# A transformer tower on one Trainium2 core: every turn of a tile by DMA, the weight preparations at other places of tile 0, and a new fixed order on all five engines

## The reference

```python
h = _L0_tok_ref(x, ...)                                  # three table rows summed, layernorm
h = h + _L0_attn_ref(_layernorm(h), ...)                 # linear attention, 16 heads, random features
h = h + _L0_ffn_ref(_layernorm(h), ...)                  # 32 prototypes, the two nearest give low-rank maps
h = h + _L1_attn_ref(_layernorm(h), ...)                 # causal softmax attention with rotary positions
h = h + _L1_ffn_ref(_layernorm(h), ...)                  # 256 -> 1024 -> 256 with ternary weights
return h
```

## Time and profile before

| | us |
|---|---|
| median of 3 runs (499.96 to 501.84) | 500.15 |
| the profiled execution | 500.82 |
| its span in the trace | 499.1 |
| TensorE busy | 394.7 |
| VectorE busy | 359.6 |
| ScalarE, GpSimd busy | 267.4, 253.5 |

### The profile page before, as it was taken

How to read it: one execution, slowest core, us unless ns; L and a number is a source line. 1 busy time by engine, 2 the same in 40 slices (tenths; PEclk the granted TensorE clock), 3 DMA queues, 4 the chain that set the end, 5 groups by cost and what they waited for, 6 DMA issues and landing times.

```text
span 499.1 us, 11429 instructions
## 1 busy us (share of the span) xinstructions
PE 394.7 (79%) x3771; PEld 262.3 (53%) x3800; DVE 359.6 (72%) x989; ACT 267.4 (54%) x579; POOL 253.5 (51%) x342
## 2 busy tenths in 40 slices
PE   3245646477889898999989999999898989868774
PEld 1032433345566564666666667666675756535432
DVE  4365479789879886889888988989796877544241
ACT  1315454154848675757667586858575655522330
POOL 6733505475757765656757485756353443411100
PEclk9765558679989997999999999999999999998899
DMA  4815904137667578767976878866978687446053
GB/s 112 253 34 167 272 11 84 32 69 123 102 110 145 103 132 158 99 127 150 161 140 141 131 156 143 169 130 134 148 120 139 111 126 131 88 96 122 16 78 93
DMA packets 194139, 60.58 MB, mean 121 GB/s; under 512 B 185696, under 2 KB 191488, under 8 KB 194080
## 3 DMA queue, kind: packets, MB, share of 16 engines
q1 hardware_dynamic: 192496, 55.52, 60.0%
q0 software_dynamic: 1584, 4.33, 3.1%
HBM read 11.85 MB, written 2.36 MB: 28 GB/s over the span
## 4 chain that ended last, share of the span: by engine, by line
PE 32%; DMA 16%; issue 15%; DVE 15%; POOL 14%; ACT 5%; SPq 3%; POOLq 0%; ACTq 0%; DVEq 0%
PE PS L1270 10%; DMA rTm<-split 6%; DVE split L960 3%; PE PS L1650 3%; DMA mT<-stage_r 3%; PE PS L1692 2%; PE PS L1605 2%; POOL qe L547 2%; DMA xTM<-xsM 2%; DMA xTo<-xso 2%; DMA qkT<-qs 2%; PE PS L1425 1%; PE PS L1593 1%; PE PS L1332 1%; POOL hres L509 1%
## 5 line engine op out<-in xcount | busy, mean ns | idle before, releaser
L1044 ACT ACTIVATE xnR<-hres,nmeanR,rstdR 128x256 f32<-128x256 f32 x16 | 9.6, 600 | 58.9 <-DVE nmeanR L937 58.9
L960 DVE TENSOR_REDUCE split<-PS 128x16 f16<-128x2048 f32 x16 | 36.7, 2292 | 4.9 <-PE PS L1583 4.9
L1650 PE MATMUL PS<-w1q,xTM 128*128 128x512 f16 x128 | 34.3, 392 | 2.9 <-DVE xTM L1008 1.7
L1692 PE MATMUL PS<-w2q,mT 128*128 128x256 f16 x256 | 31.6, 278 | 4.7 <-DMA mT<-stage_r 4.7
L1519 PE MATMUL PS<-faT_hi,hgT 128*128 128x256 f16 x128 | 24.9, 282 | 8.9 <-issue 6.3
L1280 PE MATMUL PS<-proj_hi,qkT 128*128 128x176 f16 x128 | 24.8, 256 | 7.8 <-DMA qkT<-qs 4.7
L1692 PEld LDWEIGHTS PS<-w2q,mT 128*128 128x128 f16 x256 | 24.4, 99 | 10.8 <-issue 3.7
L1270 PE MATMUL PS<-wqkT_hi,xTP 128*128 128x512 f16 x64 | 25.2, 437 | 5.5 <-DVE xTP L781 3.3
L569 POOL TENSOR_TENSOR rstdR<-rstdR,consts 128x1 f32<-128x1 f32 x16 | 8.7, 545 | 37.2 <-DVE rstdR L933 37.2
L565 POOL TENSOR_TENSOR hgs<-hg,hgs 128x512 f16<-128x512 f32 x16 | 20.8, 1298 | 12.3 <-ACT hgs L1041 12.3
L576 POOL TENSOR_TENSOR stage_f<-stage_f 128x512 f32<-128x512 f32 x16 | 20.3, 1267 | 12.9 <-DVE stage_f L955 9.4
(11 more groups left out here) (306 smaller groups left out, 1375.4 us busy)
## 6 DMA issues: line engine op xcount, KB each, us to landing
out<-outb SPq DMA_DIRECT2D x16, 128.0 KB, 2.6
w<-in_w1T SPq DMA_DIRECT2D x1, 1024.0 KB, 7.4
w<-in_w2T SPq DMA_DIRECT2D x1, 1024.0 KB, 7.8
stage_p<-in_wqkT SPq DMA_DIRECT2D x1, 512.0 KB
stage_f<-in_fbT SPq DMA_DIRECT2D x1, 512.0 KB, 4.3
stage_f<-in_faT SPq DMA_DIRECT2D x1, 512.0 KB, 4.6
stage_r<-in_rwqk SPq DMA_DIRECT2D x1, 512.0 KB, 3.9
rT<-split SPq DMA_TRANSPOSE x32, 3.3
```

Source lines behind the costliest of these rows:

```text
L960: v.tensor_reduce(slots(48)[:, 0:H, 0].rearrange("p (c j) -> p j c", j=4), PS[:, BANK["mk1"]:BANK["mk1"] + 4, :].rearrange("p j (c k) -> p ...
L1650: pe.matmul(dst, xT["M"][:, n, :], w1q[:, n % KC, cols], start=(n == 0), stop=False)
L1692: pe.matmul(PS[:, BANK["m2"], 0:D], mT[:, j, :], w2q[:, j % FC, :], start=(j == 0), stop=False)
```

## The change

The turns by TensorE at P, o, r and M are taken out with their copies (24 operations), and 24 operations of the way by DMA come in for them, on the same eight (place, tile) pairs. All numbers of the order are new, and so are the PSUM banks: `qk`, `o`, `wo`, `m2` and `pvT` share bank 2, while `Rtr`, `rqk`, `of`, `y` and `v` share bank 7; `m1`, `fK`, `fh` and `pvx` meet in banks 0 and 1, `fQ` has 4 and 5. On VectorE `setup_p` comes right behind the first normalisation of tile 0's embedding, `setup_o1` behind `Pnm` of tile 0, `setup_o2` and `setup_f1` behind its `diag`; on ScalarE `setup_o` and `setup_f` come behind `sq`, `setup_m` behind `onh`; on TensorE `setup_o2` comes behind `v` of tile 0.

```diff
-START = (2.13016, 6.2721, 10.48426, ...
+START = (12.38286, 17.45035, 22.53895, ...
 ...
-    "qk": 5, "kmxT": 2, "kbc": 2, "fK": 0, "v": 7, "ctx": 7, "fQ": 0, "o": 6,
-    "of": 7, "Ftr": 2, "prt": 0, "fh": 1, "y": 2, "Rtr": 7, "rqk": 7, "rv": 2,
-    "mk1": 3, "pvx": 6, "pvT": 2, "wo": 7, "m1": 3, "m2": 7, "Ptr": 4, "ont": 3,
-    "Mtr": 0, "rot_": 2,
+    "qk": 2, "kmxT": 6, "kbc": 6, "fK": 0, "v": 7, "ctx": 6, "fQ": 4, "o": 2,
+    "of": 7, "Ftr": 3, "prt": 3, "fh": 0, "y": 7, "Rtr": 7, "rqk": 7, "rv": 1,
+    "mk1": 3, "pvx": 0, "pvT": 2, "wo": 2, "m1": 0, "m2": 2,
 }
...
-BY_PE = {
-    "P": (0,), "o": (0, 1, 15), "M": (14, 15),
-    "r": (14, 15),
-}
...
-def taken(op, t):
-    if op in FOR_PE:
-        return t in BY_PE[FOR_PE[op]]
-    return op not in FOR_DMA or t not in BY_PE[FOR_DMA[op]]
...
     v.tensor_scalar(nmean["E"][:, :], mv["E"][:, 0:1], rstd["E"][:, 1:2], -1.0, ALU.mult, ALU.mult)\
         .then_inc(nm_ok["E"], 1)
+    if t == 0:
+        setup_p()
...
     if t == 0:
-        setup_p()
         setup_o1()
-        setup_o2()
...
     v.tensor_reduce(diag[:, :], sq[:, :, :], AX_X, ALU.add).then_inc(diag_ok, 1)
     if t == 0:
+        setup_o2()
         setup_f1()
```

More of the change, by code:

```diff
@@ L148, in place @@
         return START[t] + STRETCH[t] * PLACE[op][0 if t < FIRST else 2 if t >= LAST else 1]
-    return sorted(((op, t) for op in ENGINE[engine] for t in range(TILES) if taken(op, t)), key=lambda x: (place(*x), x[1]))
+    return sorted(((op, t) for op in ENGINE[engine] for t in range(TILES)), key=lambda x: (place(*x), x[1]))
 def wait(eng, sem, count):
@@ L1335, in step @@
             def step(op, t):
-                if op == "Ptr":
-                    wait(pe, xn_ok["P"], t + 1)
-                    free("T_P", T_ok["P"], 16 * t)
-                    free("ml2_ok", ml2_ok, issued["m1"])
-                    free("ex1_ok", ex1_ok, issued["mk1"])
-                    for c in range(KC):
-                        last = pe.transpose(PS[:, BANK["Ptr"], c * P:(c + 1) * P], xn["P"][:, c * P:(c + 1) * P], ident[:, :])
-                    last.then_inc(lo_ok["P"], 1)
-                    issued["Ptr"] = t + 1
-                elif op == "qk":
+                if op == "qk":
                     if t == 0:
@@ L1417, in step @@
                     free("ctl_ok", ctl_ok, t)
-                    free("hP_ok", hP_ok, issued["of"])
-                    free("va_ok", va_ok, issued["v"])
-                    free("hR_ok", hR_ok, issued["wo"])
-                    free("ob_ok", ob_ok, issued["m2"])
-                    free("T_R", T_ok["R"], issued["Rtr"])
-                    free("rope_ok", rope_ok, 3 * issued["rqk"])
+                    free("ex2_ok", ex2_ok, issued["mk1"])
+                    free("kb_ok", kb_ok, issued["kbc"])
+                    free("kmr_ok", kmr_ok, issued["kmxT"])
                     for j in range(HP):
@@ L1432, in step @@
                     free("on_ok", on_ok, t)
-                    free("ex2_ok", ex2_ok, issued["mk1"])
-                    free("oh_ok", oh_ok, issued["pvx"])
+                    free("sq_ok", sq_ok, issued["qk"])
+                    free("hR_ok", hR_ok, issued["wo"])
+                    free("ob_ok", ob_ok, issued["m2"])
+                    free("ro_ok", ro_ok, issued["pvT"])
                     for c, part in enumerate((cth, ctl)):
@@ L1443, in step @@
                     issued["o"] = t + 1
-                elif op == "ont":
-                    wait(pe, on_ok, t + 1)
-                    free("T_o", T_ok["o"], 16 * t)
-                    free("ml1_ok", ml1_ok, issued["m1"])
-                    free("ex1_ok", ex1_ok, issued["mk1"])
-                    for c in range(KC):
-                        last = pe.transpose(PS[:, BANK["ont"], c * P:(c + 1) * P], onorm[:, c * P:(c + 1) * P], ident[:, :])
-                    last.then_inc(lo_ok["o"], 1)
-                    issued["ont"] = t + 1
                 elif op == "of":
@@ L1509, in step @@
                     free("hF_ok", hF_ok, t)
-                    free("T_r", T_ok["r"], 16 * issued["rot_"])
-                    free("T_F", T_ok["F"], issued["Ftr"])
-                    free("vr_ok", vr_ok, issued["rv"])
-                    free("ro_ok", ro_ok, issued["pvT"])
-                    free("kb_ok", kb_ok, issued["kbc"])
-                    free("kmr_ok", kmr_ok, issued["kmxT"])
+                    free("T_R", T_ok["R"], issued["Rtr"])
+                    free("va_ok", va_ok, issued["v"])
+                    free("rope_ok", rope_ok, 3 * issued["rqk"])
+                    free("hP_ok", hP_ok, issued["of"])
                     n = R2 // P
@@ L1681, in step @@
                     free("ob_ok", ob_ok, t)
-                    free("T_R", T_ok["R"], issued["Rtr"])
-                    free("rope_ok", rope_ok, 3 * issued["rqk"])
-                    free("cth_ok", cth_ok, issued["ctx"])
-                    free("ctl_ok", ctl_ok, issued["ctx"])
-                    free("hP_ok", hP_ok, issued["of"])
-                    free("va_ok", va_ok, issued["v"])
+                    free("ro_ok", ro_ok, issued["pvT"])
+                    free("on_ok", on_ok, issued["o"])
+                    free("sq_ok", sq_ok, issued["qk"])
                     free("hR_ok", hR_ok, issued["wo"])
```

378 lines of the change are left out of this document (147 added, 231 removed), and 37 rows, old and new, of the table PLACE.

## The result

| us | before | changed |
|---|---|---|
| median | 501.0 (499.96 to 502.05, 4 runs) | 495.15 (494.76 to 497.41, 4 runs) |
| the profiled execution, its span | 500.82, 499.1 | 494.76, 493.0 |
| ratio | | 0.9893, 95% interval 0.9853 to 0.9932 |

The changed kernel is 1.1% faster: 5.9 us by the medians, 6.1 by the two spans. I had forecast 11.2. All ratios here leave out executions more than 1.5% above the fastest of their kernel and compare with the kernel before on the same chip, so the median over all executions of a run may stand higher than its ratio says.

The account below looks back on a forecast made before the run. It took TensorE as the limit only where tiles overlap (200 to 385 us), chain latency at either end. Start -1.5, filling -1.5, middle -4.2, end -4 gave -11.2 on 500.8: 489.6, said as 490, range 482 to 501.

Parts of the forecast that it names:

- The start: Tile 0's first steps: `qk` 4 us earlier, then `qT` held behind `load_w2`, a shorter way after `o`; -1.5 us.
- the middle: 200 to 385 us: TensorE's waits before `Rtr` and `of` go, a new one at `rqk` adds 2.4; -4.2 us.
- the 4.0 us go: 200 to 385 us: TensorE's 0.5 us wait before `Rtr` in eight tiles vanishes, as `wo` gets bank 2 ahead of `s2`.
- the 2.6 us go: 200 to 385 us: TensorE's wait before `of` vanishes, with 8.3 us of work after `o` instead of some 6.6.
- filling: 100 to 200 us: some 3 us of half clock on TensorE, half of it counted as going; -1.5 us.
- the half clock at 190 us: TensorE's clock at 0.66 from 190 to 200 us, taken to hold some 3 us of half clock.
- The end: Last tiles: `s1` of tile 15 3 us sooner, 1.8 us less after the last `s2`; -4.8 us walked, -4 taken.
- The gain is hidden: Rival: the start gives nothing, the middle trades its waits for others, the end gives -2; 498 us, chance 0.14.
- `m1` waits for `hg`: Rival: `m1` shares banks with `fh` and waits for `hg`, 1.2 us in each of 12 tiles; 504 us, chance 0.12.
- Late turns: Rival: at the end the DMA turns of tile 15 come too late, +5 us, the rest stands; 495 us, chance 0.12.
- 8 times 3.9: Upper bound in us on the loss from eight turns by DMA, each costing 2.4 to 3.9 more on the path.
- most are beside the path: Claim that most of the eight turns changed to DMA lie off the path that sets the time; no size given.

Follow-up runs that it names:

- a_w2_late: The changed kernel with `load_w2` moved from behind `PT` of tile 1 to behind `load_w1`: ratio 0.9859 to the kernel before, median 492.9 us.
- a_fill_Rtr: The changed kernel with two filler matmuls on TensorE ahead of `Rtr` of tiles 4 to 11: ratio 0.9902 to the kernel before, median 495.1 us.
- b_wo_early: The kernel before, with TensorE issuing `wo` ahead of `s2` in the rounds of `s2` 4 to 11: ratio 1.0062.
- a_turn_pe0: The changed kernel with the turns of r of tile 15 and M of tiles 14 and 15 back on TensorE: ratio 0.9938 to the kernel before, median 496.6 us.

## Why the prediction was right and wrong

**Right in direction, half in size.** Faster was forecast at 0.75, and 495.15 lies in the range; the time itself is 5 us too low.

**The start was sized right, in part by luck.** -1.4 us at `hP` of tile 0 against my -1.5, and most of its steps hold: `qk` of tile 0 at 33.35 (32.5 to 33), `qT` issued at 41.05 (41), the product at 48.44 (47.5). But `o` came at 62.1 (60.7), 1.4 us late where I had said no gain, and from `o` to `hP` it took 8.1 us instead of 10.6, 2.5 less where I had counted 1.5. The figure taken from the row, 6.1 us for a transpose behind loads, came close: it took 7.4, and `a_w2_late` shows that the load is the cause. The fit in the Trainium skill ("DMA: Bandwidth & Descriptors", section "Anatomy of one DMA") gave an estimate of 46 for the landing of `qT`. The trace does not agree, with the product at 48.44, and the measurement decides.

**The step that failed is the middle: "the 4.0 us go", "the 2.6 us go", counted in full.** They went, and the time did not: in the 185 us TensorE idles 10.2 us instead of 11.5, since other waits came. In my sum each us in which TensorE did not wait was a us of time, because TensorE is busy 94% there. `a_fill_Rtr` shows what such a us is worth in this order: 3.5 us put in, none of it seen in eight rounds. `b_wo_early` shows in the old order that a wait can be taken out without a gain: 4.0 us of it went, 7.3 us of another came with the move, and 0.6% was lost. The medians have -1.5 us instead of -4.2, and +0.4 for the stage of the **filling** instead of -1.5, so these two terms brought 1.1 us of the 5.7 I had counted. These 4.6 us are most of the gap of 5.3 (11.2 to 5.9), as far as medians of stages can say that spread by 5 to 7 us. What paces the middle instead stays open.

The filling failed in another way. It rested on the half clock at 190 us, which lies behind `hP` of tile 4 and so counts in the table's third row. It did go in the changed kernel's trace, but other traces of the changed order have such a stretch close by: 0.66 from 180 to 190 us in `a_turn_pe0`, 0.83 from 175 to 185 in `a_w2_late`. So it looks like chance of the execution, and I had counted half of it as a gain.

**The end came near, but not by the way I walked.** At like clock it gave 2.5 us up to `ngm` of tile 15 and 2.5 from there, 5 us against my -4 (-4.8 by the walk). After the last `s2` it is -1.6 (34.3 to 32.7 us), said -1.8, with 1.4 us lost at half clock in it. Ahead of it I had `s1` of tile 15 3 us sooner, counted from `rqk` of that tile; it is 13.6 us from one to the other, where it was 14.1, so only 0.5 us came there and the rest earlier, by steps I did not name. `s2` of tile 15 starts at 459.71, 4.5 us earlier than before, not 7 to 9. I had also missed that tile 13 comes late on TensorE and on GpSimd; the two edits that mend this brought nothing that can be measured.

**The rivals.** "The gain is hidden" (498) named what came true for the middle: waits traded for others. I gave it 0.14, since the waits "have a cause by bank and order that is gone". The cause was gone; it proved nothing of the time. "`m1` waits for `hg`" did not come in any row. "Late turns" did not come either, since the `mT` chain covers them. I had also put the loss of eight turns at 8 times 3.9 at the most, and had taken "most are beside the path"; in the old order they cost 9 us, part of it by their place in the queue, which a price per turn does not hold.

## To carry to other kernels

A wait in the profile of a busy engine is worth its length only if nothing else holds up the same stretch. Put a filler of that length at the same place first: if the time does not grow, there is slack at that place, and taking the wait away is not likely to help. Where all transposes share one queue, the price of one more is its place: see what stands ahead of it and when that gets its data. Where half clock falls differs between executions, so compare stages with it apart from stages without it. Compare stages over several traces of programs that are alike there before giving a cause to 2 us.
